# Another table of turns (issue orders) for a fused vision-transformer, Mamba and expert kernel

## The reference

```python
h = tok(x)                            # patch embedding, 2 x (attention + gated feed-forward), rmsnorm
h = layernorm(h + mamba_f(h) + flip(mamba_b(flip(h))))
h = layernorm(h + experts(h))         # top 8 of 64, the first 256 rows of each expert kept
# mamba: dA = exp(dt*A); h[t] = dA[t]*h[t-1] + dt*B[t]*x[t]; y = sum_s h*C + D*x; y*silu(z)
```

## Time and profile before

| | before |
|---|---|
| median of 3 runs | 8892.51 us (8873.36 to 8898.86) |
| profiled execution, its own time | 8887.31 us |
| profiled execution, span first to last instruction | 8885.5 us |
| PE / DVE / ACT busy, share of the span | 79% / 79% / 70% |
| mean granted TensorE clock | 0.925 |

### The profile page before, as it was taken

One profiled execution on the slowest core, in us unless ns is written; L12 is line 12 of the kernel. 1 busy time (PEld: TensorE's weight loads), 2 busy tenths in 40 slices (PEclk: granted clock), 3 DMA queues, 4 the chain that ended last, 5 costly groups with the idle time before them and its releaser, 6 DMA issues. The chain is left out here.

```text
span 8885.5 us, 117469 instructions
## 1 busy us (share of the span) xinstructions
PE 7020.2 (79%) x33290; PEld 3894.5 (44%) x33290; DVE 7053.6 (79%) x9195; ACT 6179.2 (70%) x13424; POOL 806.7 (9%) x554
## 2 busy tenths in 40 slices
PE   6777777788888888888888888888888888888561
PEld 3444444444444444444444444444444444444330
DVE  2788888888888888888888888888888888888743
ACT  4766666677777777777777777777777777777434
POOL 0133333400000000000000000000000000000055
PEclk8988989899999999999999999999999999999775
DMA  2233333233333323333333333333333333332356
GB/s 91 105 119 119 109 109 108 92 118 117 115 120 117 118 107 123 114 119 114 115 117 115 114 115 121 113 112 115 121 117 109 122 115 117 111 122 109 127 116 199
DMA packets 282498, 1034.03 MB, mean 116 GB/s; under 512 B 37570, under 2 KB 129526, under 8 KB 273824
## 3 DMA queue, kind: packets, MB, share of 16 engines
q1 hardware_dynamic: 248352, 1009.77, 31.6%
q0 software_dynamic: 33792, 21.18, 1.5%
HBM read 951.57 MB, written 90.94 MB: 117 GB/s over the span
## 5 line engine op out<-in xcount | busy, mean ns | idle before, releaser
L1047 PE MATMUL psS<-KM,Q 128*99 128x394 f32 x4096 | 1718.4, 536 | 351.2 <-ACT PTs L578 260.8
L843 DVE TENSOR_TENSOR_SCAN hs<-dA,hs 128x1576 f32<-128x1576 f32 x512 | 1762.3, 3442 | 63.0
L572 ACT ACTIVATE P<-psS,least_s 99x197 f32<-99x197 f32 x4096 | 1413.4, 431 | 469.4 <-DVE least_s L768 466.3
L1054 PE MATMUL psS<-cst,P 99*99 99x99 f32 x8192 | 1047.9, 268 | 345.1 <-ACT P L572 300.6
L1054 PEld LDWEIGHTS psS<-cst,P 99*99 99x99 f32 x8192 | 912.2, 176 | 895.9 <-ACT P L572 654.5
L768 DVE TENSOR_REDUCE least_s<-psS 99x2 f32<-99x394 f32 x2048 | 1087.7, 562 | 261.7 <-PE psS L1047 229.6
L649 ACT ACTIVATE dA<-dt_,aneg 128x394 f32<-128x394 f32 x2048 | 1184.4, 621 | 28.9 <-DVE hs L843 18.9
L578 ACT ACTIVATE PTs<-psS 99x396 f32<-99x396 f32 x2048 | 985.9, 517 | 223.6 <-PE psS L1054 219.0
L1047 PEld LDWEIGHTS psS<-KM,Q 128*99 128x99 f32 x4096 | 626.4, 174 | 1086.9 <-ACT PTs L578 578.0
L829 DVE TENSOR_TENSOR hs<-hs,u 128x1576 f32<-128x1576 f32 x512 | 917.6, 1792 | 42.2 <-DMA hs<-bc_scratch 40.7
L1139 PE MATMUL psY<-hs,cst 128*128 128x394 f32 x2048 | 831.4, 536 | 116.1 <-DVE hs L852 115.7
(11 more groups left out here) (214 smaller groups left out, 9499.9 us busy)
## 6 DMA issues: line engine op xcount, KB each, us to landing
hs<-bc_scratch SPq DMA_DIRECT2D x512, 788.0 KB
cr<-bc_scratch SPq DMA_DIRECT2D x512, 788.0 KB
pat<-patches SPq DMA_DIRECT2D x64, 1176.0 KB, 5.9
more_scratch<-zeros SPq DMA_DIRECT2D x64, 197.0 KB, 5.2
rows_scratch<-hs SPq DMA_DIRECT2D x1, 12352.0 KB, 43.1
PTs<-more_scratch SPq DMA_DIRECT2D x24, 512.0 KB
sum_scratch<-HW SPq DMA_DIRECT2D x64, 148.5 KB
hs<-rows_scratch SPq DMA_DIRECT2D x24, 386.0 KB
```

The source lines that it names most:

```text
L572: last = nc.scalar.activation(P[:, r, b, m, 0:T], psS[0:CT, 2 * r + b, m * T:(m + 1) * T], ACT.Exp, bias=least_s[:, r, b, m:m + 1], scale= ...
L843: nc.vector.tensor_tensor_scan(h, a, h, 0.0, ALU.mult, ALU.add).then_inc(scan_ready, 1)
L1047: mm(psS[0:CT, 2 * r + b, 0:2 * T].rearrange("p (e t) -> p e t", e=2), Q[:, r, b, q * CT:(q + 1) * CT], KM[:, r, h % 2 * 2:h % 2 * 2 + 2, ...
L1054: last = nc.tensor.transpose(psS[0:CT, 2 * r + b, at:at + CT], P[:, r, b, m, k * CT:(k + 1) * CT], c("ident")[0:CT, 0:CT])
```

## The change

Both tables are replaced, STAGES (an order of the same 101 stages) and PLACE (the stage behind which each of the 104 units is put, for each engine). Operations, buffers, semaphores, UNITS and `loop` are the same. The numbers are long lists, so the diff is shown by the ends of the lists:

```diff
-STAGES = [('square', 1, 0), ('norm', 1, 0), ('conv', 0), ('square', 0, 0), ('qkv', 1), ('keys', 1, 0), ('norm', 0, 0), ('score', 1, 0, 0), ('qkv', 0), ('keys', 0, 0), ('score', 1, 0, 1), ('keys', 1, 1), ('turn', 1, 0, 0), ('score', 0, 0, 0), ('turn', 1, 0, 1), ('score', 0, 0, 1), ('score', 1, 1, 0), ('score', 1, 1, 1),
...
-  ('up', 0), ('down', 1), ('down', 0), ('square', 1, 2), ('norm', 1, 2)]
+STAGES = [('square', 1, 0), ('norm', 1, 0), ('conv', 0), ('square', 0, 0), ('qkv', 1), ('keys', 1, 0), ('norm', 0, 0), ('score', 1, 0, 0), ('score', 1, 0, 1), ('qkv', 0), ('keys', 0, 0), ('keys', 1, 1), ('turn', 1, 0, 0), ('turn', 1, 0, 1), ('score', 0, 0, 0), ('score', 1, 1, 0), ('score', 1, 1, 1), ('score', 0, 0, 1),
...
+  ('up', 0), ('down', 1), ('square', 1, 2), ('norm', 1, 2), ('down', 0)]
-PLACE = {'dve': [18, 0, 0, 0, 13, 0, 4, 0, 0, 2,
...
+PLACE = {'dve': [0, 0, 0, 7, 0, 0, 0, 6, 6, 4,
...
```

More of the change, by code:

```diff
@@ L82, in role_stages @@
     return out
-STAGES = [('square', 1, 0), ('norm', 1, 0), ('conv', 0), ('square', 0, 0), ('qkv', 1), ('keys', 1, 0), ('norm', 0, 0), ('score', 1, 0, 0), ('qkv', 0), ('keys', 0, 0), ('score', 1, 0, 1), ('keys', 1, 1), ('turn', 1, 0, 0), ('score', 0, 0, 0), ('turn', 1, 0, 1), ('score', 0, 0, 1), ('score', 1, 1, 0), ('score', 1, 1, 1), ('turn', 1, 1, 0), ('keys', 0, 1), ('turn', 0, 0, 0), ('turn', 1, 1, 1), ('turn', 0, 0, 1), ('score', 0, 1, 0), ('score', 0, 1, 1), ('score', 1, 2, 0), ('turn', 0, 1, 0), ('score', 1, 2, 1), ('turn', 0, 1, 1), ('score', 0, 2, 0), ('score', 0, 2, 1), ('keys', 1, 2), ('turn', 1, 2, 0), ('turn', 1, 2, 1), ('keys', 0, 2), ('turn', 0, 2, 0), ('turn', 0, 2, 1), ('score', 1, 3, 0), ('score', 0, 3, 0), ('score', 0, 3, 1), ('keys', 0, 3), ('score', 1, 3, 1), ('turn', 0, 3, 0), ('turn', 0, 3, 1), ('keys', 1, 3), ('turn', 1, 3, 0), ('turn', 1, 3, 1), ('value', 0, 0), ('value', 1, 0), ('score', 1, 4, 0), ('score', 1, 4, 1), ('score', 0, 4, 0), ('score', 0, 4, 1), ('turn', 1, 4, 0), ('turn', 0, 4, 0), ('turn', 1, 4, 1), ('turn', 0, 4, 1), ('score', 1, 5, 0), ('score', 0, 5, 0), ('score', 0, 5, 1), ('score', 1, 5, 1), ('turn', 1, 5, 0), ('turn', 1, 5, 1), ('turn', 0, 5, 0), ('turn', 0, 5, 1), ('score', 1, 6, 0), ('score', 1, 6, 1), ('score', 0, 6, 0), ('score', 0, 6, 1), ('turn', 1, 6, 0), ('turn', 1, 6, 1), ('turn', 0, 6, 0), ('turn', 0, 6, 1), ('score', 1, 7, 0), ('score', 0, 7, 0), ('score', 0, 7, 1), ('score', 1, 7, 1), ('turn', 1, 7, 0), ('turn', 1, 7, 1), ('turn', 0, 7, 0), ('turn', 0, 7, 1), ('value', 1, 1), ('value', 0, 1), ('den', 1), ('den', 0), ('wo', 1), ('wo', 0), ('square', 1, 1), ('square', 0, 1), ('norm', 1, 1), ('norm', 0, 1), ('gate', 1), ('gate', 0), ('sig', 1), ('sig', 0), ('up', 1), ('up', 0), ('down', 1), ('down', 0), ('square', 1, 2), ('norm', 1, 2)]
@@ L87 @@
-PLACE = {'dve': [18, 0, 0, 0, 13, 0, 4, 0, 0, 2, 1, 1, 4, 6, 19, 9, 10, 15, 19, 18, 61, 14, 27, 9, 21, 17, 21, 0, 22, 25, 28, 11, 34, 34, 2, 8, 5, 16, 0, 35, 0, 44, 0, 46, 0, 4, 1, 0, 47, 6, 48, 48, 48, 54, 2, 6, 11, 8, 56, 12, 56, 14, 57, 44, 62, 62, 7, 1, 63, 20, 47, 35, 20, 66, 72, 72, 72, 66, 80, 80, 80, 12, 9, 6, 80, 82, 9, 82, 67, 90, 91, 7, 97, 73, 1, 4, 0, 13, 12, 97, 0, 0, 0, 19], 'act': [6, 0, 2, 1, 15, 0, 1, 1, 2, 2, 10, 1, 13, 0, 0, 6, 9, 6, 14, 20, 22, 24, 14, 30, 27, 4, 4, 0, 0, 22, 5, 3, 49, 6, 1, 28, 28, 36, 36, 18, 10, 21, 0, 13, 40, 43, 43, 43, 0, 8, 0, 46, 2, 2, 48, 56, 56, 61, 6, 23, 51, 79, 60, 73, 100, 0, 57, 62, 0, 64, 64, 72, 78, 9, 63, 0, 0, 62, 69, 0, 0, 78, 77, 61, 0, 0, 55, 81, 48, 74, 76, 28, 88, 86, 95, 95, 95, 12, 16, 1, 96, 96, 96, 99], 'pe': [6, 0, 0, 1, 14, 0, 2, 9, 4, 13, 0, 0, 8, 2, 17, 13, 40, 39, 1, 2, 30, 4, 12, 36, 23, 10, 5, 35, 0, 46, 51, 23, 1, 4, 37, 30, 0, 0, 2, 0, 11, 44, 42, 7, 4, 27, 22, 29, 3, 6, 9, 47, 0, 6, 9, 0, 0, 7, 0, 55, 55, 37, 60, 17, 46, 10, 69, 64, 0, 42, 79, 92, 94, 9, 67, 14, 6, 77, 99, 3, 0, 78, 92, 81, 7, 0, 94, 79, 11, 20, 4, 94, 0, 5, 11, 21, 0, 0, 0, 0, 0, 0, 4, 0], 'sp': [17, 12, 31, 74, 43, 8, 12, 12, 8, 8, 17, 8, 21, 13, 44, 39, 51, 48, 53, 19, 11, 70, 96, 86, 96, 93, 55, 79, 19, 38, 47, 93, 50, 34, 22, 38, 20, 30, 38, 33, 100, 75, 68, 67, 60, 56, 69, 46, 21, 100, 18, 67, 46, 52, 72, 95, 90, 87, 28, 100, 100, 100, 99, 100, 96, 88, 90, 88, 96, 90, 90, 82, 87, 87, 87, 81, 87, 91, 92, 89, 70, 95, 100, 92, 22, 46, 91, 79, 100, 87, 61, 11, 79, 90, 44, 47, 0, 100, 100, 5, 33, 44, 53, 69]}
@@ new lines @@
+STAGES = [('square', 1, 0), ('norm', 1, 0), ('conv', 0), ('square', 0, 0), ('qkv', 1), ('keys', 1, 0), ('norm', 0, 0), ('score', 1, 0, 0), ('score', 1, 0, 1), ('qkv', 0), ('keys', 0, 0), ('keys', 1, 1), ('turn', 1, 0, 0), ('turn', 1, 0, 1), ('score', 0, 0, 0), ('score', 1, 1, 0), ('score', 1, 1, 1), ('score', 0, 0, 1), ('turn', 1, 1, 0), ('keys', 0, 1), ('turn', 0, 0, 0), ('turn', 0, 0, 1), ('turn', 1, 1, 1), ('score', 0, 1, 0), ('score', 0, 1, 1), ('score', 1, 2, 0), ('turn', 0, 1, 0), ('score', 1, 2, 1), ('turn', 0, 1, 1), ('keys', 1, 2), ('score', 0, 2, 0), ('score', 0, 2, 1), ('turn', 1, 2, 0), ('turn', 1, 2, 1), ('keys', 0, 2), ('turn', 0, 2, 0), ('turn', 0, 2, 1), ('score', 1, 3, 0), ('score', 1, 3, 1), ('score', 0, 3, 0), ('score', 0, 3, 1), ('keys', 0, 3), ('turn', 0, 3, 0), ('turn', 0, 3, 1), ('keys', 1, 3), ('turn', 1, 3, 0), ('turn', 1, 3, 1), ('value', 0, 0), ('value', 1, 0), ('score', 1, 4, 0), ('score', 0, 4, 0), ('score', 0, 4, 1), ('score', 1, 4, 1), ('turn', 1, 4, 0), ('turn', 0, 4, 0), ('turn', 0, 4, 1), ('turn', 1, 4, 1), ('score', 1, 5, 0), ('score', 0, 5, 0), ('score', 0, 5, 1), ('score', 1, 5, 1), ('turn', 1, 5, 0), ('turn', 1, 5, 1), ('turn', 0, 5, 0), ('turn', 0, 5, 1), ('score', 1, 6, 0), ('score', 0, 6, 0), ('score', 1, 6, 1), ('score', 0, 6, 1), ('turn', 1, 6, 0), ('turn', 1, 6, 1), ('turn', 0, 6, 0), ('turn', 0, 6, 1), ('score', 1, 7, 0), ('score', 1, 7, 1), ('score', 0, 7, 0), ('score', 0, 7, 1), ('turn', 1, 7, 0), ('turn', 1, 7, 1), ('turn', 0, 7, 0), ('turn', 0, 7, 1), ('value', 1, 1), ('value', 0, 1), ('den', 1), ('den', 0), ('wo', 1), ('square', 1, 1), ('wo', 0), ('square', 0, 1), ('norm', 1, 1), ('norm', 0, 1), ('gate', 1), ('gate', 0), ('sig', 1), ('sig', 0), ('up', 1), ('up', 0), ('down', 1), ('square', 1, 2), ('norm', 1, 2), ('down', 0)]
@@ new lines @@
+PLACE = {'dve': [0, 0, 0, 7, 0, 0, 0, 6, 6, 4, 1, 2, 2, 2, 9, 8, 11, 48, 63, 70, 38, 11, 17, 55, 0, 19, 19, 7, 22, 25, 29, 3, 31, 35, 4, 18, 3, 0, 0, 35, 26, 37, 9, 48, 33, 26, 24, 29, 48, 11, 48, 48, 51, 56, 23, 28, 16, 23, 56, 2, 56, 6, 40, 79, 60, 62, 20, 2, 62, 6, 4, 22, 43, 67, 69, 69, 70, 51, 74, 81, 81, 2, 21, 3, 82, 82, 18, 82, 70, 90, 91, 4, 93, 32, 6, 10, 7, 4, 10, 98, 19, 9, 7, 30], 'act': [0, 0, 0, 1, 11, 0, 1, 1, 2, 2, 1, 1, 2, 9, 40, 6, 0, 6, 6, 13, 21, 2, 18, 82, 7, 4, 6, 10, 0, 21, 2, 0, 32, 8, 15, 29, 32, 34, 37, 0, 32, 8, 28, 20, 43, 43, 45, 45, 0, 19, 3, 46, 32, 10, 46, 56, 60, 63, 3, 2, 46, 70, 60, 97, 74, 0, 72, 62, 3, 67, 67, 69, 78, 6, 63, 3, 0, 94, 70, 1, 0, 78, 71, 18, 0, 0, 94, 81, 57, 32, 5, 0, 92, 90, 95, 96, 97, 23, 19, 8, 97, 97, 97, 97], 'pe': [4, 0, 0, 1, 11, 0, 1, 8, 9, 5, 6, 4, 2, 4, 9, 3, 15, 90, 53, 83, 67, 0, 14, 48, 21, 29, 0, 25, 4, 63, 53, 20, 37, 2, 37, 1, 8, 11, 10, 2, 52, 6, 40, 18, 28, 35, 17, 0, 0, 31, 3, 47, 21, 31, 20, 41, 2, 18, 0, 33, 52, 27, 60, 74, 39, 0, 71, 63, 8, 23, 17, 61, 80, 12, 79, 2, 0, 84, 79, 15, 0, 78, 100, 81, 0, 0, 92, 24, 17, 0, 2, 92, 0, 0, 0, 3, 2, 10, 9, 0, 21, 7, 0, 39], 'sp': [14, 12, 40, 96, 100, 37, 45, 17, 25, 28, 82, 64, 72, 72, 87, 77, 39, 69, 66, 24, 16, 11, 48, 100, 69, 65, 44, 49, 39, 35, 36, 100, 46, 28, 28, 34, 34, 33, 30, 31, 100, 79, 24, 67, 43, 22, 31, 24, 21, 100, 31, 65, 76, 76, 81, 85, 46, 53, 35, 53, 50, 100, 89, 100, 51, 22, 53, 37, 24, 70, 30, 69, 78, 70, 69, 78, 72, 64, 77, 71, 10, 27, 100, 80, 2, 48, 98, 79, 100, 85, 21, 7, 69, 91, 50, 62, 25, 100, 100, 32, 59, 38, 34, 46]}
```

## The result

| | before | after |
|---|---|---|
| median of 5 runs each | 8876.67 us (8868.21 to 8898.86) | 8837.69 us (8816.2 to 8841.11) |
| ratio, 95% interval | | 0.9941 (0.992 to 0.9962) |
| span of the profiled execution | 8885.5 us | 8835.9 us |
| mean granted TensorE clock | 0.925 | 0.918 |

What follows compares the result with a forecast made beforehand. A turn was taken as DVE's work plus its gaps. Gains of 1.7 + 0.8 + 0.2 = 2.7 us a turn, times 61 = 165 us, took the profiled 8887.3 us to 8722 us; stated range 8660 to 8845.

Steps and rivals of the forecast that it cites:

- Place A: Across the turn's edge: norm's matmul between the two downs, DVE gaps 3.95 to 2.25 us, worth 1.7 us a turn.
- I take the high level, so project(0,0) ends at 4318.1: At the turn's edge: down(0) fills PE's hole, so project(0,0) runs at the high clock; otherwise it ends 1.8 us later.
- ACT's loop edge: ACT's 2.30 us idleness before its first square, moving to 4316.7; hidden if project(0,0) ends after 4317.3.
- The walk: Stepping the new queues through one turn with the old operation lengths; turns of about 123.6 us.
- Place B: Just after the merge: DVE's waits for round 5 scores shrink, 0.8 us a turn, the same in routing turns.
- Place C: Ahead of wo: sum(1), 1.5 us, moves into PE's 2.4 us wait for DVE, worth 0.2 us a turn.
- the same queue around them: 0: Merge (3.2 us), gate chain and load of input(0) (0.5) keep their surrounding queue, so no change.
- Rival 1: Clock stays low at project(0,0): 1.0 us a turn won, 8826 us; chance 0.2.
- Rival 2: Gaps only move, as ACT, 74% busy, becomes the late one: about 0.2 us a turn, 8875 us; chance 0.1.
- Rival 3: Slower: block of four scores behind output(5) is exposed, deciding past 4.35 us a turn; 8948 us at 5.3; chance 0.1.

Runs made afterwards that it cites:

- the main part of the edit, alone: Kernel before with down(0) moved behind the last norm in all queues and the last decay of group 5 ahead of ACT's square: 8778.21 us, ratio 0.9885.
- the routing's part: Kernel before with only the routing moved earlier on PE and ACT, and the unit -leave earlier on PE: 8808.14 us, one run.
- its two parts alone: Kernel before with down(0) behind the last norm and the routing earlier on PE and ACT: 8708.35 us, ratio 0.9799.
- The added matmuls: Kernel after with eleven unused matmuls of 394 columns a turn in five waits of PE: 8625.85 us, ratio 0.9712.
- The control: Kernel after with the same eleven added matmuls at the same places, 16 columns each instead of 394: 8843.23 us, ratio 0.996.

## Why the prediction was right or wrong

- **Place A, 1.7 us: right.** 3.95 us of waits became 1.9 in the turn read, and the main part of the edit, alone, gave 1.5 a turn. The step "I take the high level, so project(0,0) ends at 4318.1" held (2.91 us for eight matmuls), and ACT's loop edge stayed hidden (its first square starts at 4270.02, before project(0,0) ends). The walk took the last norm's own wait on DVE to stay; it grew by 0.5 us a turn, as much as ys(0) won ahead of sig(0).
- **Place B, 0.8: right in late turns, too small in turns with routing.** Round 5 no longer waits; alone, on the old table, the routing's part gave 0.6 in late turns (one run). In early turns it gave 3.9 where 0.8 had been forecast. That the early turns of the new table are 2.7 us shorter, as forecast, is luck: its two parts alone give 3.5 there, and the rest of the table takes 0.8 away.
- **Place C, 0.2: right in its place, nil in the turn.** Moving sum(1) into the hole shortens wo's waits by 0.9 us a turn against the same table without the move, and the merge, the scores and the load take 0.8 back. Against the kernel before, wo waits 0.3 longer all the same, as its matmuls run more often at the low clock (599 ns on average, 552 before).
- **The step that failed** is "the same queue around them: 0" for the merge and the load, together with the scores between round 1 and input(0), which the sum left as they were. The clock was costed at project(0,0) only, and elsewhere taken to stay as before because PE would wait as long as before. But from round 1 to the merge PE's queue is another one: the sum of group 5 is ahead of its old place, one hole is 2.50 us long instead of 1.92, and the low clock lasts some 10 us instead of 3. DVE pays for it with 0.8 us a turn more ahead of scores, 1.0 at the merge, 0.3 at wo and 0.3 for the load, 2.4 in all, where the sum had 0 or less. In 48 turns that gave back what A and B had won. The added matmuls show that PE's clock is the cause: with them the turn is 122.7 us, and with 16 columns in place of 394 it is 126.2. (122.7 is 0.9 under the 123.6 of the walk, but that does not confirm the walk, as the added matmuls also remove low stretches that the kernel before had.) Which move of the table makes PE late at the merge stays open; the sum of group 5 put back explains the scores, and neither the merge nor the lost time.
- **Rival 1** came nearest in time (8826), by another mechanism: the clock stayed high where it said low, and was low where nothing had been forecast. **Rival 2**, gaps that only move, is what happened in kind, but it named ACT as the cause, and matmuls in PE's waits, with ACT's order as it was, removed the loss. **Rival 3**: the block of scores costs 1.33 us, far from the 4.35 at which it would decide.

The Trainium skill (TensorE: Matmul & The Clock Gate, Part 1) says that the slow clock is the default and activity releases it. The control agrees: eleven full matmuls a turn took the mean granted clock from 0.918 to 0.957, the same eleven with 16 columns to 0.924. The prediction used this rule at one hole and had to use it at all of them.

## What to carry to other kernels

Where several engines share a turn and none is full, read PE's holes and the granted clock behind each, not DVE's waits alone: an order that moves matmuls out of a thin stretch can lose on the clock what it wins in waits. A sum over places must also price the places between them: here each single gain was real where it was forecast, and moving sum(5), sum(1) or the routing alone each made a wait elsewhere longer. A reordering should be tried part by part; here one moved stage and one earlier branch (8708 us) beat the full new table (8838 us). And if a hole cannot be closed, idle matmuls into a bank that nobody reads can pay: eleven a turn took the kernel after from 8838 to 8626 us, the fastest of all. They are no sure gain: twelve a turn on the old table gave 8821 us, 0.7%, and a low stretch came up elsewhere.

## What the runs showed of the hardware

More work for PE shortened the time. From the kernel after to the same with all eleven added matmuls, PE's busy time in window 4000:6000 rose from 1692 to 1785 us, the granted clock from 0.95 to 0.99 and DVE's work done in it from 1666 to 1711 us:

```profile
4000.00:6000.00 2000.00, 1692.12 (x7991) 947.77 (x7989) 1666.40 (x1984) 1476.76 (x3221) 8.27 (x16) 0.95 0.32 116
```
```profile
4000.00:6000.00 2000.00, 1784.50 (x8612) 985.05 (x8611) 1710.78 (x2037) 1517.10 (x3305) 8.28 (x16) 0.99 0.33 119
```

The mean clock of the whole run tells little: after, it is lower than before (0.918 against 0.925) in a faster kernel. It matters which matmuls are slow, those that DVE waits for or others.
